# Expert stages of a language-model tower: up matmuls of two steps, then down matmuls of two steps, over six rotating PSUM banks

## The reference, cut to what matters

```python
def _L1_ffn_ref(x, Wg, bg, W1, b1, W2, b2):
    B, S, D, H, E, K = (8, 2048, 64, 256, 8, 2)
    gate_scores = jnp.einsum('bsd,ed->bse', x, Wg) + bg
    topk_scores, topk_idx = jax.lax.top_k(gate_scores, K)
    topk_probs = jax.nn.softmax(topk_scores, axis=-1)
    combine = jnp.sum(topk_probs[..., None] * jax.nn.one_hot(topk_idx, E, dtype=x.dtype), axis=-2)
    out = jnp.zeros_like(x)
    for e in range(E):
        h = jax.nn.relu(jnp.einsum('bsd,hd->bsh', x, W1[e]) + b1[e])
        y = jnp.einsum('bsh,dh->bsd', h, W2[e]) + b2[e]
        out = out + combine[..., e:e + 1] * y
    return out
...
h = h + _L0_attn_ref(_layernorm(h, axis=-1), ...)
h = h + _L0_ffn_ref(_layernorm(h, axis=-1), ...)
h = h + _L1_attn_ref(_layernorm(h, axis=-1), ...)
h = h + _L1_ffn_ref(_layernorm(h, axis=-1), ...)
```

## Time and profile before

| | us |
|---|---|
| median of three runs | 598.67 |
| the three runs | 598.67, 600.78, 596.02 |
| span of the profiled execution | 593.9 |
| PE busy in it | 534.8 |
| ACT busy | 381.5 |
| DVE busy | 413.9 |

### The profile page before, as it was taken

One profiled execution on the slowest core, in us unless ns is written; L12 is line 12 of the kernel. 1 busy time (PEld: TensorE's weight loads), 2 busy tenths in 40 slices (PEclk: granted clock), 3 DMA queues, 4 the chain that ended last, 5 costly groups with the idle time before them and its releaser, 6 DMA issues.

```text
span 593.9 us, 8251 instructions
## 1 busy us (share of the span) xinstructions
PE 534.8 (90%) x2798; PEld 279.4 (47%) x2798; DVE 413.9 (70%) x1114; ACT 381.5 (64%) x619; POOL 16.9 (3%) x29
## 2 busy tenths in 40 slices
PE   1898899999999997779999999999847999999995
PEld 1555685334333333656666676666524333333331
DVE  6887797566627555898999999999876336334343
ACT  0379746655666653448888887888734656765653
POOL 4060000000000000000000000000000000000000
PEclk9989998999999998979999999999988999999998
DMA  7910010422131313000000000000000312222220
GB/s 202 252 26 1 6 49 1 128 53 72 37 93 43 95 59 106 1 1 1 1 1 1 1 2 1 1 1 1 1 1 4 108 54 72 76 81 81 69 89 18
DMA packets 26840, 28.08 MB, mean 47 GB/s; under 512 B 12240, under 2 KB 17392, under 8 KB 26736
## 3 DMA queue, kind: packets, MB, share of 16 engines
q1 hardware_dynamic: 24496, 26.98, 16.1%
q10 hardware_dynamic: 2304, 0.58, 0.6%
HBM read 26.24 MB, written 1.31 MB: 46 GB/s over the span
## 4 chain that ended last, share of the span: by engine, by line
PE 51%; DVE 32%; issue 6%; ACT 6%; DMA 3%; SPq 1%; DVEq 0%; ACTq 0%
PE bank L1509 21%; PE bank L1520 20%; DVE l1mom L1240 3%; DVE Xs L1233 3%; DMA Ph<-in_itok 2%; PE bank L1355 2%; DVE Xn L1265 2%; DVE small L1201 2%; DVE Cen L1246 2%; DVE Mm L1226 1%; DVE ksm L1170 1%; DVE Ph L1195 1%; DVE small L1189 1%; ACT Hd L735 1%; PE bank L1422 1%
## 5 line engine op out<-in xcount | busy, mean ns | idle before, releaser
L647 ACT ACTIVATE Hd<-bank,b1all 128x512 f32<-128x512 f32 x256 | 154.9, 688 | 89.0 <-PE bank L1509 88.9
L1520 PE MATMUL bank<-Hd,w2m 128*64 128x512 f32 x512 | 123.7, 605 | 0.9 <-DVE Rest L1084 0.9
L1084 DVE SCALAR_TENSOR_TENSOR Tmp<-bank,b2col,Wb 128x512 f32<-128x512 f32 x56 | 42.0, 750 | 105.7 <-PE bank L1520 104.8
L1520 PEld LDWEIGHTS bank<-Hd,w2m 128*64 128x64 f32 x512 | 31.2, 136 | 85.9 <-issue 80.3
L1509 PE MATMUL bank<-Ph,w1m 64*128 64x512 f32 x256 | 65.2, 628 | 1.3 <-DVE Sc L1015 1.3
L1509 PE MATMUL bank<-XT,w1m 64*128 64x512 f32 x256 | 65.3, 625 | 0.0
L735 ACT ACTIVATE Hd<-bank,lvecs 128x512 f32<-128x512 f32 x64 | 38.7, 688 | 3.3 <-PE bank L1678 3.1
L1509 PEld LDWEIGHTS bank<-XT,w1m 64*128 64x128 f32 x256 | 23.0, 190 | 37.5 <-issue 18.9
L1629 PE MATMUL bank<-bd,XT 128*128 128x128 f32 x256 | 35.9, 285 | 5.2 <-ACT Hd L735 5.1
L1629 PEld LDWEIGHTS bank<-bd,XT 128*128 128x128 f32 x256 | 32.0, 196 | 17.8 <-ACT Hd L735 16.8
L1088 DVE TENSOR_TENSOR Rest<-Rest,Tmp 128x512 f32<-128x512 f32 x56 | 38.7, 692 | 1.9
(11 more groups left out here) (212 smaller groups left out, 825.6 us busy)
## 6 DMA issues: line engine op xcount, KB each, us to landing
Wb<-gate_rows SPq DMA_DIRECT2D x128, 128.0 KB, 2.9
Ph<-in_x SPq DMA_DIRECT2D x4, 512.0 KB, 9.3
Ph<-in_itok SPq DMA_DIRECT2D x4, 384.0 KB, 10.0
w1m<-in_w1e SPq DMA_DIRECT2D x1, 1028.0 KB, 19.2
w2m<-in_w2e SPq DMA_DIRECT2D x2, 512.0 KB, 13.7
w1m<-in_w1e SPq DMA_DIRECT2D x1, 1024.0 KB, 5.5
out<-Hs SPq DMA_DIRECT2D x16, 64.0 KB, 2.1
Hd<-in_w1all SPq DMA_DIRECT2D x1, 512.0 KB, 15.0
```

The source lines that it names most:

```text
L647: ac.activation(Hd[:, st.ring, k // 2, k % 2, :], bank[k][:, :], func, bias=b1all[:, st.m, st.e, k // 2:k // 2 + 1]).then_inc(up_read, 1)
L1084: ve.scalar_tensor_tensor(dst, bank[st.down_bank][:, :], b2, Wb[:, st.t % RING, :], ALU.add, ALU.mult).then_inc(down_read, 1)
L1520: ins = te.matmul(bank[st.down_bank][h * D:(h + 1) * D, :], w2m[:, st.e, hc * D:(hc + 1) * D], Hd[:, st.ring, hc, h, :], start=(hc == 0), ...
```

## The change

The loops over steps become loops over batches. `BATCHES` is [0], [1], [2, 3], [4, 5] and so on to [30, 31]. PE does the up parts of the next batch, then the down parts of this one, then the side work. The results of up parts take the three pairs of banks (0, 1), (2, 3), (4, 5) in turn, and most of the side work's results take a pair of the same rotation (`beside`); down results go to banks 6 and 7. `up_made` and `up_read` are gone: the up results are users of `PsumPlan` as all else. The hidden results have four places, two in Hd and two in a part of Ph that is free in these stages (`HdB`). Side work is moved by up to a few steps, so that it stands behind an odd step. `experts_in` waits for all eight banks.

```diff
@@
+import itertools
 from contextlib import ExitStack
 import concourse.bass as bass
@@
+STEPS = G * E
+BATCHES = [[0], [1]] + [[n, n + 1] for n in range(2, STEPS, 2)]
+
+
 class PsumPlan:
@@
     def put(what, *places):
         for *key, b in places:
             plan.add((what, *key), b)
+
+    pairs = itertools.cycle(((0, 1), (2, 3), (4, 5)))
+
+    def beside(*keys):
+
+        for key, b in zip(keys, next(pairs)):
+            plan.add(key, b)
+
+    def ups(m, batch):
+        for n in batch:
+            for hc in range(2):
+                beside(*(("up", m, n, 2 * hc + h) for h in range(2)))
     def quarters(what, g, *banks):
         for n, b in enumerate(banks):
@@
     put("gate", (0, 0, 7))
     put("xe", (0, 0, 1), (0, 1, 6))
     plan.at["before experts", 0] = list(plan.count)
+    ups(0, BATCHES[0])
     put("ret", (3, 7))
-    put("ct", (0, 0, 6), (0, 1, 7))
-    put("xt", (1, 2, 6), (1, 3, 7))
-    put("o0", (2, 6), (3, 7))
-    put("xm", (0, 2, 6), (0, 3, 7))
-    put("at", (0, 0, 6))
-    put("gate", (0, 1, 7))
-    put("xe", (0, 2, 6), (0, 3, 7))
-    put("ct", (0, 2, 6), (0, 3, 7))
-    put("at", (0, 1, 6), (0, 2, 7), (0, 3, 6))
+    for i, batch in enumerate(BATCHES):
+        ups(0, BATCHES[i + 1] if batch[-1] < STEPS - 1 else ())
+        if batch[-1] == 9:
+            beside(("gate", 0, 1))
+        if batch[-1] == 0:
+            beside(("ct", 0, 0), ("ct", 0, 1))
+        if batch[-1] == 1:
+            beside(("xt", 1, 2), ("xt", 1, 3))
+        if batch[-1] == 3:
+            beside(("o0", 2), ("o0", 3))
+        if batch[-1] == 7:
+            beside(("xm", 0, 2), ("xm", 0, 3))
+        if batch[-1] == 9:
+            beside(("xe", 0, 2), ("xe", 0, 3))
+        if batch[-1] == 11:
+            beside(("ct", 0, 2), ("ct", 0, 3))
+        if batch[-1] in (13, 17, 25):
+            beside(("at", 0, (batch[-1] - 9) // E))
+    put("at", (0, 3, 6))
     put("xm", (1, 0, 4), (1, 1, 5))
     put("gate", (1, 0, 4))
     put("ct", (1, 0, 6), (1, 1, 7))
     plan.at["before experts", 1] = list(plan.count)
-    put("xm", (1, 2, 6), (1, 3, 7))
-    put("gate", (1, 1, 6))
-    put("at", (1, 0, 7))
-    put("ct", (1, 2, 6), (1, 3, 7))
-    put("at", (1, 1, 6), (1, 2, 7), (1, 3, 6))
+    ups(1, BATCHES[0])
+    for i, batch in enumerate(BATCHES):
+        ups(1, BATCHES[i + 1] if batch[-1] < STEPS - 1 else ())
+        if batch[-1] == 1:
+            beside(("xm", 1, 2), ("xm", 1, 3))
+        if batch[-1] == 3:
+            beside(("gate", 1, 1))
+        if batch[-1] == 7:
+            beside(("ct", 1, 2), ("ct", 1, 3))
+        if batch[-1] in (9, 17, 25):
+            beside(("at", 1, (batch[-1] - 9) // E))
+    put("at", (1, 3, 6))
     return plan.at
-
-
-STEPS = G * E
 class Step:
@@
         self.g, self.e = n // E, n % E
         self.t = STEPS * m + n
         self.ring = n % 2
-        self.down_bank = 5 - self.ring
+        self.down_bank = 6 + self.ring
         self.first = self.t < 2
-        self.very_first = self.t == 0
         self.opens = self.e == 0
         self.added = self.t - self.t // E
@@
         Hd = sb("Hd", [P, 2, 2, 2, GC])
+        HdB = Ph[:, 0:2, :].rearrange("p r (c h n) -> p r c h n", c=2, h=2)
         XE = Ph[:, 3, :]
         Acc = Rest
@@
         gap_ready, tanh_ready = sem("gap_ready"), sem("tanh_ready")
         w1_scaled, comb_ready, b1_in = sem("w1_scaled"), sem("comb_ready"), sem("b1_in")
-        up_made, up_read = sem("up_made"), sem("up_read")
         wb_in = [sem(f"wb_in{r}") for r in range(RING)]
         rows_out = [sem(f"rows_out{g}") for g in range(G)]
         down_made, down_read, acc_done = sem("down_made"), sem("down_read"), sem("acc_done")
@@
         def mean_count(k, part):
             return [key for key in ln_order if key[0] != 3].index((k, part)) + 1
+
+        def hidden_of(st):
+
+            return (Hd, HdB)[st.n // 2 % 2][:, st.ring, :, :, :]
         def gslice(g):
             return slice(g * GC, (g + 1) * GC)
@@
                         store((n - 14) // E)
             all_gates(0)
-            sp.wait_ge(up_made, 4 * STEPS)
             sp.wait_ge(down_made, STEPS)
             expert_weights(1)
             all_gates(1)
@@
             def hidden(st):
                 func = ACT.Gelu if st.m == 0 else ACT.Relu
                 for k in range(4):
-                    act.wait_ge(up_made, 4 * st.t + k + 1)
-                    ac.activation(Hd[:, st.ring, k // 2, k % 2, :], bank[k][:, :], func,
-                                  bias=b1all[:, st.m, st.e, k // 2:k // 2 + 1]).then_inc(up_read, 1)
+                    key = ("up", st.m, st.n, k)
+                    full(act, key)
+                    read(ac.activation(hidden_of(st)[:, k // 2, k % 2, :], ps(key)[:, :], func,
+                                       bias=b1all[:, st.m, st.e, k // 2:k // 2 + 1]), key)
             xt_out(0, 0)
             xt_out(0, 1)
@@
                 if n == 9:
                     turned_out(0, 2)
                     turned_out(0, 3)
-                if n == 12:
+                if n == 11:
                     operand_out(2)
                     operand_out(3)
+                    tanh_gap(0, 1)
                 if n == 13:
-                    tanh_gap(0, 1)
-                if n == 15:
                     weights_out(0, 1)
             act.wait_ge(l1_in, L1_DMAS * 16)
             scale = float(DH) ** -0.25
@@
                 if n == 3:
                     turned_out(1, 2)
                     turned_out(1, 3)
+                if n == 7:
+                    tanh_gap(1, 1)
                 if n == 9:
-                    tanh_gap(1, 1)
-                if n == 13:
                     weights_out(1, 1)
@@
             norm_retrieved(1)
             for n in range(STEPS):
                 weigh(Step(0, n))
-                if n == 4:
+                if n == 3:
                     attended(1)
-                if n == 5:
                     attended_in(1)
                     layernorm(2, 1, Hs, Xs)
-                if n == 6:
+                if n == 5:
                     operand_norm(1)
-                if n == 10:
+                if n == 7:
+                    routed(0, 1)
+                if n == 9:
+                    route_weights(0, 1)
+                if n == 13:
                     mixed(0, 0)
-                    routed(0, 1)
-                if n == 12:
-                    route_weights(0, 1)
-                if n == 18:
+                if n == 17:
                     mixed(0, 1)
                     mixed_in(0, 0)
                     layernorm(4, 0, Hs, Xs)
-                if n == 22:
+                if n == 21:
                     first_norms(0)
-                if n == 26:
+                if n == 25:
                     mixed(0, 2)
                     taken(dve, ("at", 0, 2))
-                if n == 27:
                     layernorm(4, 2, Hs, Xs)
-                if n == 30:
+                if n == 29:
                     first_norms(2)
             mixed(0, 3)
@@
             layernorm(5, 1, Hs, Xn)
             for n in range(STEPS):
                 weigh(Step(1, n))
+                if n == 3:
+                    routed(1, 1)
                 if n == 5:
-                    routed(1, 1)
-                if n == 8:
                     route_weights(1, 1)
-                if n == 10:
+                if n == 9:
                     mixed(1, 0)
-                if n == 18:
+                if n == 17:
                     mixed(1, 1)
-                if n == 26:
+                if n == 25:
                     mixed(1, 2)
             mixed(1, 3)
@@
                 taken(pe, ("xe" if m == 0 else "xm", m, g))
-            def up(st):
-                operand = XE if st.m == 0 else XT
-                for k in range(4):
-                    hs = slice(k % 2 * D, (k % 2 + 1) * D)
-                    if not st.very_first:
-
-                        pe.wait_ge(up_read, 4 * st.t + k - 3)
-                    te.matmul(bank[k][:, :], w1m[hs, st.e, k // 2 * P:(k // 2 + 1) * P],
-                              operand[hs, gslice(st.g)], start=True, stop=True).then_inc(up_made, 1)
-
-            def down(st):
-                if not st.first:
-
-                    pe.wait_ge(down_read, st.t - 1)
-
-                pe.wait_ge(up_read, 4 * st.t + 4)
-                for hc in range(2):
-                    for h in range(2):
-                        ins = te.matmul(bank[st.down_bank][h * D:(h + 1) * D, :],
-                                        w2m[:, st.e, hc * D:(hc + 1) * D],
-                                        Hd[:, st.ring, hc, h, :], start=(hc == 0), stop=(hc == 1))
-                ins.then_inc(down_made, 1)
+            def up(m, batch):
+                operand = XE if m == 0 else XT
+                for st in (Step(m, n) for n in batch):
+                    if st.n and st.opens:
+                        operand_in(m, st.g)
+                    for k in range(4):
```

(66 more changed lines are left out.)

## The result

| | before | after |
|---|---|---|
| median, us | 597.35 (4 runs) | 589.50 (4 runs) |
| runs, us | 595.54 to 600.78 | 586.73 to 591.89 |
| span of the profiled execution | 593.9 | 590.1 |
| its own time | not listed | 591.89 |

What follows compares the result with a forecast made beforehand. PE alone was taken to bound the expert stages; terms -10.2 + 1.2 + 0.1 - 0.9 - 0.4 - 0.2 = -10.4 took the span from 593.9 to 583.5, with 4.8 around it 588.3 us, range 584 to 592.

Steps and rivals of the forecast that it cites:

- What bounds the stages: Expert stages: only PE counts, idling 0.9 and 0.0 us; a microsecond taken from its sequence comes off the end.
- The batches: Both expert stages: 30 pairs of tiling changes fall away at 0.34 us each, saving 10.2 us (8.7 to 11).
- The margin of 0.04 us: Batch's fourth up pair reuses banks ACT has read 0.04 us earlier: cost 0; rival of ACT setting the pace 0.13, 596.7.
- DVE at the shared banks: Up part after a lone `at`: third pair waits 0.2 us for DVE's `mixed` at six places, +1.2 us (0 to 3).
- The rival that DVE is late there: Ten DVE-read results share banks with up; from 1.7 us late at each, the kernel is over 1% slower, 605; chance 0.05.
- More waits: A down part waits for four `psum_free` counts instead of one `up_read`: cost 0, at most 13 us if nothing hid them.
- "+0.1": First stage's start: `experts_in` also waits for the gate scores' bank, read until 92.48, up(0) started at 92.49: +0.1 us.
- the wait for the copies of `ct`: Second stage's start: up(0) begins 0.8 us later, but six banks speed the following up parts at half clock: -0.2 together.
- The stall of down(2): First stage: down(2) stood 0.93 us for weigh(0); up(4), up(5) and two transposes now lie before it: -0.9 us.
- the end of the first stage: PE's wait until weigh(31) is shortened, not removed, as `first_norms(2)` moves ahead of weigh(30): -0.4 us.

Runs made afterwards that it cites:

- the run with one tiling: Changed kernel with batches of one step, and second-stage down matmuls in the up matmuls' tiling (used for times alone): 595.27 us, one run.
- The four-bank run: Changed kernel with up results in banks 0 to 3 alone and side work in 4 and 5: 620.91 us.
- the one with six banks: Changed kernel, but the entry to a stage waits for banks 0 to 5 alone: median 586.89 us, ratio to before 0.9801.
- single steps: Changed kernel with batches of one step each; banks, side work and waits as in the changed kernel: 602.24 us, ratio to before 1.0068.
- the kernel before with eight: Kernel before with one edit, the entry to a stage waits for all eight banks: 598.81 us beside 597.65, ratio 1.0040.
- the four of the changed kernel with six banks: Changed kernel waiting for six banks: alone 586.89 us; with inner turn_back before down parts 583.66; with one wait per down part 584.35; with all three edits 583.55.
- retrieve later: Changed kernel (all eight banks at the start) with retrieve(3) after up(1) in place of before it: 587.66 us, ratio to before 0.9808.
- The last kernel (six banks): Changed kernel with six banks at stage starts, turn_back before down parts, one wait per down part, and retrieve(3) after up(1): 583.73 us, ratio 0.9738.

## Why the prediction was right, point by point

**What bounds the stages.** Right. The chain of waits between the stages' starts and ends is still PE alone, and what was taken from PE's sequence came off the end.

**The batches.** The term was 0.34 us for each of 30 pairs of changes, 10.2. Measured in the ordinary batch: 7.56 - 7.21 = 0.35, 10.5. The cause was argued from differences of starts and the row of down(31); the run with one tiling showed it. How the prediction divides the 0.34 does not hold: it puts 0.20 after an up part and 0.14 after a down part. In the trace of before, single matmul records inside a part follow each other every 0.42 us; at the change from up to down the two gaps around it are 0.52 and 0.47, and at the change back 0.52 and 0.53. So the way from up to down costs 0.15 and the way back 0.20. The sum takes both together, so it is not touched.

**ACT.** The margin of 0.04 us held. No up part waits for ACT in matmul time, only a weight load does. The four-bank run shows that the arithmetic behind this margin holds: 4.7 us worked out, 4.69 measured.

**DVE at the shared banks.** Predicted 0.2 us at six places, measured 0.17 at the same six. The rival that DVE is late there didn't come about: `mixed` stands ahead of each layernorm, not behind.

**More waits.** Taken at 0 in the down parts, and 0 they are. At the start of the stages this was wrong: see the next point.

**The starts of the stages.** Here the sum failed. In the first, "+0.1" for the wait for the gate scores' bank was 0.57: behind its last mask DVE reads the bank (0.21), and then 0.56 us pass to the first matmul, where the kernel before and the one with six banks need 0.20 in all. In the second, the wait for the copies of `ct` was taken as 0.8 and measured as 1.0: from DVE's Xs to up(0) 2.75 us in place of 1.74. What I had not in the sum at all is the clock: I took the half-speed stretch for as long as in the profile before, and at the same place in the trace, and it grew from 3.4 to 13.6 and from 3.4 to 6.8 us. From up(0) to down(0) of the second stage it is 6.16 us in place of 5.63, where the sum had 1.0 less. By the four points above the sum had +0.1, -5.8, -0.2 and -4.5, together -10.4; the profiles have +5.2, -6.1, +2.0 and -4.9, together -3.8. So the starts lost 5.1 and 2.2 us against the sum, and the stages gave back 0.3 and 0.4: 6.6, the gap between 583.5 and 590.1. Of the 2.2, 0.5 are in the beats themselves, which no edit touched.

**The stall of down(2) and the end of the first stage.** Right: the changed kernel has no wait of PE behind weigh(0), and PE's wait at the end is 3.48 us, where it was 3.75 (229.65 to 233.40). From down(0) to the beats the sum said 5.1 + 0.9 + 0.4 - 0.6 = 5.8 us less, and it is 6.1. For the second stage 4.5 and 4.9.

**The median.** 588.3 against 589.5 is in part luck. Two errors met: the clock's loss was left out, and 4.8 us were put around the span, taken from the median of before, where the profiled execution has 591.89 - 590.1 = 1.8. If before has the same 1.8, the other 3.0 are what its profiled execution was faster than the median. With the sum's span and 1.8 the time would have been 585.3; runs near it exist (585.99, 586.73), but none of them was profiled.

## What to carry to other kernels

Two kinds of matmul that tile the array differently cost time at each change between them, here 0.15 and 0.20 us; read it as the difference between the start-to-start times of parts and the spacing inside a part, and put as many of one kind together as PSUM lets you. How many it lets you is arithmetic from rows: when the reader of the first bank is done, against when the next turn of that bank comes. And a wait added at the entry of a dense stage, where the engine's clock is low, may cost more than its own length: look at how long the low stretch lasts, what runs in it, and in how many executions it is long, because one profile shows one of them.

## What the runs showed of the hardware

- A change from 64*128 to 128*64 tiling costs 0.15 us of start-to-start time and the way back 0.20; with one tiling both are 0 (1.72 us per part of eight records in both). The time lies around the change: the gap ahead of it and the gap behind the first new matmul are both longer than the 0.42 us inside a part.
- PE's granted clock fell to half (1.2 GHz) between 89.1 and 92.3 us, among gate matmuls, transposes and waits of up to 1.9 us ahead of up(0), and stayed there for 3.4, 6.8, 13.6 or 17.1 us, with matmuls running for most of it (12.55 of 13.60 us in the changed kernel). With retrieve(3) in its old place, all five profiles of kernels with eight banks at the start have 13.6 us or more at the start of the first stage (the changed kernel, single steps, one tiling, four banks for up, and the kernel before with eight), the four of the changed kernel with six banks have 6.8, and the kernel before has 3.4.
- In the second stage the stretch at up(0) is 6.8 us in the profiles of the changed kernel, single steps, one tiling, four banks and retrieve later, all with eight banks, and 3.4 in that of before and in the four with six banks. The last kernel (six banks) and the kernel before with eight had a stretch of 17.1 us in the beats ahead instead; the second of them then had 6.8 more. What sets these lengths beyond the two edits tried stays open.
- PE needed 0.20 us from the release to the first up matmul with the wait for six banks, and 0.56 to 0.71 with the wait for all eight. Which of its waiting instructions takes this time was not tried.
